# k's remainder taken from PSUM, and an earlier place for Pool's residual addition

## What is computed

```python
def _mlp(x, W1, b1, W2, b2):
    h = jax.nn.gelu(x @ W1 + b1, approximate=False)
    return h @ W2 + b2

# attention, without a softmax
q, k, v = _mlp(x, W1q, ...), _mlp(x, W1k, ...), _mlp(x, W1v, ...)
scores = jnp.einsum('bid,bjd->bij', q, k) / sqrt(256 * 512) * tril
out = jnp.einsum('bij,bjd->bid', scores, v)
out = layernorm(out) * ln_w + ln_b

# feed forward: the position of a row picks one of 8 matrices
idx = argmax(pe @ sign(tile_sigs).T)
y = x @ W[idx].T + b[idx]

x = x + attention(layernorm(x))
x = x + feed_forward(layernorm(x))
```

## Time and profile before

| | |
|---|---|
| median of 3 runs | 330.68 us (329.66 to 331.28) |
| profiled execution | 329.83 us, its span 328.1 us |
| PE busy | 281.4 us (86%) |
| DVE, ACT, POOL busy | 232.0, 202.5, 196.8 us |
| chain that ended last | PE 63%, DVE 17%, POOL 5%, issue 5%, ACT 5%, DMA 3% |
| starts of steps 1 to 6 (first transposes) | 69.04, 100.84, 131.62, 163.76, 193.40, 223.06 us |

### The profile page before, as it was taken

The page is one execution under the profiler, slowest core; times in us unless marked ns, Lnnn a source line. Parts: engine busy times, 40 slices in busy tenths (PEclk is TensorE's granted clock), DMA queues, the critical chain, the costliest instruction groups (busy, mean ns, idle before and its releaser), DMA issues.

```text
span 328.1 us, 5585 instructions
## 1 busy us (share of the span) xinstructions
PE 281.4 (86%) x1828; PEld 252.1 (77%) x1828; DVE 232.0 (71%) x538; ACT 202.5 (62%) x402; POOL 196.8 (60%) x227
## 2 busy tenths in 40 slices
PE   5899999799989998899899999999998969996000
PEld 5778988698779888787878898899887969996000
DVE  3799759778987768865876787679569798885000
ACT  2377576667566884587468856966774469991000
POOL 3533506451664787589638854964793557777772
PEclk9579999999999999999999999999999999999555
DMA  8806940200020012001201040100047414943210
GB/s 213 284 0 212 337 156 1 67 31 0 2 91 8 32 65 98 32 33 34 97 2 47 20 128 16 51 1 2 32 122 193 125 53 137 306 145 112 75 54 2
DMA packets 24656, 28.01 MB, mean 85 GB/s; under 512 B 4722, under 2 KB 22386, under 8 KB 24564
## 3 DMA queue, kind: packets, MB, share of 16 engines
q1 hardware_dynamic: 15764, 13.07, 13.6%
q0 software_dynamic: 3488, 8.99, 7.8%
q10 hardware_dynamic: 5376, 5.59, 5.4%
HBM read 13.99 MB, written 14.56 MB: 87 GB/s over the span
## 4 chain that ended last, share of the span: by engine, by line
PE 63%; DVE 17%; POOL 5%; issue 5%; ACT 5%; DMA 3%; POOLq 0%; SPq 0%; DVEq 0%; ACTq 0%
PE ring L427 35%; PE o_ps L427 9%; PE s_ps L427 6%; POOL out_dram L1477 5%; PE sc_ps L427 4%; DMA w_stage<-w1k 3%; PE w_ps L427 2%; DVE xres L1004 2%; PE ring L440 2%; PE ring L669 2%; PE ring L518 1%; DVE hT L930 1%; DVE state L976 1%; DVE kT L942 1%; DVE v L955 1%
## 5 line engine op out<-in xcount | busy, mean ns | idle before, releaser
L427 PE MATMUL ring<-xnT,w_sp 128*128 128x512 f32 x288 | 75.1, 408 | 3.1 <-DVE xnT L925 1.7
L427 PEld LDWEIGHTS ring<-xnT,w_sp 128*128 128x128 f32 x288 | 54.0, 195 | 15.6 <-issue 2.0
L427 PE MATMUL ring<-hT,w_sp 128*128 128x512 f32 x192 | 47.4, 398 | 4.5 <-DVE qT L936 3.0
L726 ACT ACTIVATE h<-ring,b_cols 128x512 f32<-128x512 f32 x48 | 33.0, 687 | 21.1 <-PE ring L427 20.7
L427 PEld LDWEIGHTS ring<-hT,w_sp 128*128 128x128 f32 x192 | 35.0, 188 | 14.2 <-DVE qT L936 4.1
L1392 POOL DMA_INDIRECT sorted_rows<-xres,slot_i x32 | 33.8, 1057 | 8.6 <-issue 6.1
L1356 POOL TENSOR_TENSOR hT<-h,hT 128x512 fp32r<-128x512 f32 x24 | 31.7, 1331 | 4.5 <-ACT hT L729 4.3
L1362 POOL TENSOR_TENSOR vtok<-v,vtok 128x512 fp32r<-128x512 f32 x14 | 17.7, 1284 | 23.8 <-ACT vtok L749 23.8
L1381 POOL TENSOR_TENSOR xres<-ve,half 128x4 f32<-128x4 f32 (+1 forms) x9 | 8.7, 968 | 37.2 <-DVE ve L1024 37.1
L729 ACT CAST hT<-h 128x512 fp32r<-128x512 f32 x48 | 29.8, 620 | 1.5
L976 DVE TENSOR_TENSOR state<-s_ps,state 128x512 fp32r<-128x512 f32 x27 | 18.6, 688 | 16.5 <-ACT state L768 16.5
(11 more groups left out here) (181 smaller groups left out, 635.8 us busy)
## 6 DMA issues: line engine op xcount, KB each, us to landing
sorted_rows<-blank ACTq DMA_DIRECT2D x1, 5070.0 KB, 20.3
xt<-x SPq DMA_DIRECT2D x8, 512.0 KB, 3.6
slot_rows<-sorted_rows SPq DMA_DIRECT2D x23, 130.0 KB, 4.0
h<-sorted_rows SPq DMA_DIRECT2D x16, 130.0 KB, 2.7
w_stage<-tile_w SPq DMA_DIRECT2D x8, 256.0 KB, 4.0
hT<-position_table POOLq DMA_DIRECT2D x1, 512.0 KB, 7.1
sorted_rows<-xres,slot_i POOLq DMA_INDIRECT x32, 2.7
row_stage<-rows ACTq DMA_DIRECT2D x1, 384.0 KB, 8.1
```

Source lines behind the costliest of these rows:

```text
L427: last = te.matmul(o, lhs[k][a], rhs[k][c], start=start and k == 0 and i == 0, stop=stop and k == n - 1 and i == 2, skip_group_check=check)
L726: nc.scalar.activation(h32[:, m, :], ring[(2 + m) % 3][:, :], ACT.Gelu, bias=b1c[:, m // 2, m % 2:m % 2 + 1]).then_inc(gelu, 1)
```

## The change

`k_rest` reads k from its PSUM bank and adds the bias itself, as `q_rest` does; so the two instructions of TensorE that write those banks next wait for `k_lo` instead of `k_full`. ACT still writes `k32`. Pool's `residual(s + 1)` moves from behind `rstd_out` to behind h1's remainder, in the branch for steps 0, 1, 3, 4, 5 and 6.

```diff
 def front_v(s, first):
...
-                        te.wait_ge(k_full, 2 * s + 1)
+                        te.wait_ge(k_lo, 2 * s + 1)
...
 def front_ktok(s):
...
-                        te.wait_ge(k_full, 2 * s + 2)
+                        te.wait_ge(k_lo, 2 * s + 2)
...
 def k_rest(s, j):
     dve.wait_ge(k_hi, 2 * s + 1 + j)
-    nc.vector.tensor_tensor(kT[:, 1, j, :], k32[:, j, :], kT[:, 0, j, :].bitcast(F32),
-                            ALU.subtract).then_inc(k_lo, 1)
+    nc.vector.scalar_tensor_tensor(out=kT[:, 1, j, :], in0=ring[(10 + j) % 3][:, :],
+                                   scalar=b2c[:, K, j:j + 1], in1=kT[:, 0, j, :].bitcast(F32),
+                                   op0=ALU.add, op1=ALU.subtract).then_inc(k_lo, 1)
...
                     h_rest(s + 1, 1)
+                    residual(s + 1)
                     if s > 2:
                         rows_sorted(s - 1, (2, 3))
                     h_rest(s + 1, 3)
                     h_rest(s + 1, 5)
                     rstd_out(s)
-                    residual(s + 1)
                     if s + 1 < LAST:
                         v_rest(s + 1)
```

## The result

The changed kernel takes 341.99 us (median of 4 runs, 341.17 to 342.13) against 330.17 us before on the same chip: 3.5% slower, ratio 1.0349 (95% interval 1.0313 to 1.0385). The profiled execution has a span of 340.3 us against 328.1. The forecast was 338.4 us with a range of 332.5 to 341.5: right in sign and in the waits that it found, 3.6 us short, and 0.5 us outside the range.

A forecast was written before the change was run, and what follows sets the result against it. TensorE, busy 281.4 of 328.1 us, was taken as the bound; step terms 2.3 + 3.1 + 0 + 1.05 + 0.6 + 0.6 + 0 = +7.7 us took 329.83 to 337.5, plus 0.85 for the median: 338.4 us, range 332.5 to 341.5.

The forecast's parts named there:

- Part 1: `k_rest` from PSUM: 0.69 to about 0.75 us each, stretched ones become normal; gain up to 1.5 us in step 3.
- step 3: Pass ending block 3: k0 delayed at least 2.5 us by the residual on Pool, transposes later by +1.05 us.
- The new waits: On TensorE, v's second half and first `ktok` group wait for `k_lo`: slack 0.5 us or more, or covered by other waits.
- Step 0: Pass ending block 0: Pool's reads hold DVE's routing instructions, h2 comes late and TensorE waits: +2.3 us.
- Steps 4 and 5: Passes ending blocks 4 and 5: Pool's h3, behind residual and scatters, delays TensorE's k0: 0.6 us lost in each.
- Step 1: Pass ending block 1: DVE's `route_slots` instructions held by Pool, h2 and q's remainder late for TensorE: +3.1 us.
- rival (d): TensorE's clock halves after idling some 3.3 us in steps 1 and 3: +4 to 5 us, about 342.5; 8 in 100.
- (a): DVE's tiny routing instructions pass beside Pool, so steps 0 and 1 cost nothing: 333.0 us; 14 in 100.
- (b): Pool's delay is hidden since TensorE doesn't wait for h3: -0.5 to -1.5 us, 329.7, no difference; 11 in 100.
- (c): Faster: freed h4 and `k_rest` let ACT and DVE run ahead in steps 4 to 6: about 328.4 us; 5 in 100.

The follow-up runs named there:

- k_only: Changed kernel with the residual back in its old place in every step, `k_rest` still reading PSUM: 329.29 us, ratio 0.9972.
- write_only: `k_only` plus four Pool memsets in steps 0 and 1 where the changed kernel has the residual: 333.31 us, ratio 1.0093.
- write_no_copy: `write_only` with two copies in DVE's routing made as a maximum of the value with itself: 328.21 us, ratio 0.9939.
- rows_behind: Changed kernel with the two row scatters of steps 3 to 6 moved behind h5's remainder: 338.9 us.
- after_warm: Changed kernel with 22 purposeless TensorE transposes ahead of the k products in steps 1 and 3: 339.09 us.
- res_only: Changed kernel with `k_rest` and its semaphores as in the kernel before, residual early: 342.29 us, ratio 1.0347.
- after_route_late: Changed kernel with DVE's routing arithmetic of steps 0 and 1 after the remainders of h2 and h4: 338.31 us.

## Why the prediction was wrong where it was

- **Part 1**: right. `k_rest` takes 739 to 751 ns in all 16 places, step 3 gains 0.6 us and the kernel 0.9 (expected of `k_only` were 0.5 to 1.5). The new waits came as worked out: nothing in steps 0, 1, 4 and 5, 1.26 us in step 2 in the place of the wait for v, and 0.58 us in step 6, under ACT's. (Its sum for `k_rest` in step 5, 6.5 us, comes to 6.35; the slack only grows.)
- **Step 0** (+2.3, measured +2.4): right down to the instructions. L1086, L1089 and L1090 of the kernel before were held for 2.47, 1.19 and 1.19 us. `write_only` and `write_no_copy` show that it is the reading Pool instruction that holds them: beside memsets in the same place they run free.
- **Steps 4 and 5** (+0.6, measured +1.0 and +0.9): the mechanism is shown by `rows_behind`. The term was short by two small ones. The first scatter took 1.29 us and not 1.04, since DVE's h2, let go by the residual at 221.8, ran in it (that the one slowed the other is argued from the times). And k0 had been due earlier than the working took it: it counted from 210.98, where the chain has the q products, but the timeline has them start at 210.82 and twelve of them take 2.80 us, so k0 was due at 213.62 and not at 213.80.

```profile
219.56 2.79 DVE L930 TENSOR_TENSOR hT<-h,hT 128x512 fp32r<-128x512 f32 x1
...
221.96 1.29 POOL L1393 DMA_INDIRECT sorted_rows<-xres,slot_i  x1 [0.17 <-issue]
```

- **Step 1** (+3.1, measured +5.2) and **step 3** (+1.05, measured +2.8): here it failed. The waits ahead of k0 were found: k0 came 3.2 us later in step 1, and 2.8 in step 3, where the working had "2.5 us at least" (the residual took 2.77 us there and not 2.40). The step that failed is the one from these waits to the time: the sum counts every matmul behind them at full clock, and puts the clock at nothing. The clock went into rival (d), at 8 in 100 and priced outside the range, for the reason that "no idleness as long is seen inside the loop". In its place the runs show that TensorE's clock fell to half in both steps (2.93 us for k1 where 1.65 was taken, 4.46 for twelve k products where 3.01 was), and `after_warm` prices that at 1.9 and 1.4 us, 3.3 of the 4.5 us that the sum lacks. The prediction's own text had rightly said that TensorE would idle 3.3 us there. It then held for unlikely what the trace didn't show, when the long idleness that the trace did show had ended with a fallen clock. (TensorE's last matmuls start at 299.59 and take 0.88 us, so it stopped at 300.5 and not at 299.8.) The rival's price of 4 to 5 us was too high, because the clock came back during v.
- **The rivals**: (a) fell, no tiny instruction passed beyond one per Pool instruction. (b) fell, Pool's h3 was what TensorE waited for in steps 3 to 5. (c) fell. (d) came true on top of the forecast's waits.
- **The Trainium skill**: "SBUF — State Buffer", section "Who interferes with whom", has two rules that bear on this. One is that a DVE instruction with two SBUF inputs contends with a GpSimd instruction that reads SBUF and not with one that only writes it. The traces agree: 0.19 to 0.22 us beside the memsets of `write_only`, 1.19 to 2.47 us beside the reads of the changed kernel. The other is that copies and casts can enter modes that use the shared port pair, and can then contend. That agrees with the copy's 1.96 us beside memsets, and the expectation of `write_only` had not used it.

## What to carry to other kernels

Moving a long Pool instruction away from the DVE instruction that it holds only helps if the new place holds nothing: list every DVE instruction with two SBUF inputs beside the new place, and everything behind it on Pool, and ask for each who waits. An idle stretch of TensorE that a change creates can cost more than its length, since the clock may be half afterwards: here the long ones cost 1.4 and 1.9 us on top. Cutting the long instruction in four, in its old place, shortened its hold on DVE from 2.2 to 0.55 us and step 2 by 1.7 us.

## What was not expected of the hardware

- A wait of 2.82 us ahead of k0 halved TensorE's clock in `rows_behind` and left it full in `res_only`; 2.37 us (`write_only`) left it full, and 3.37 to 3.55 us halved it in each profile. It then stayed down for 3.4 to 6.8 us, and in step 3 the same twelve products took 4.46, 4.58 or 5.46 us.
- A DVE copy of 8 elements was held 1.8 us by Pool memsets that read nothing, through the seams between four of them, while two-input instructions of the same size were not held.
- A held two-input instruction of 16 to 96 elements got in between two Pool instructions in a row each time (steps 0 and 1 of the changed kernel). One of 512 elements, h4's remainder, did not in the kernel before (2.28 us, through h3 and h5), but did in `after_route_late` between the residual and h3 (1.60 us, and the two Pool instructions after it took 2.98 us, not 2.54). What decides is open.
